# Second attention of a two-layer kernel: rotary rows of the next group exchanged and turned in two halves, at lower steps of the group

## The reference, cut to what matters

```python
q = rmsnorm(hidden_states @ wq_a.T, q_a_ln_w) @ wq_b.T       # 192 per head: 128 nope + 64 rotary
q_nope, q_pe = (q[..., :NOPE], q[..., NOPE:])
q_pe = apply_rope(q_pe, cos, sin)                            # x * cos + rot(x) * sin
q_abs = jnp.einsum('bhsd,hdc->bhsc', q_nope, q_absorb)       # 64 latent rows per head
scores = (jnp.einsum('bhsc,btc->bhst', q_abs, kv) + jnp.einsum('bhsd,bxtd->bhst', q_pe, k_pe)) * SCALE
attn = jax.nn.softmax(jnp.where(causal, scores, finfo.min), axis=-1)
x = jnp.einsum('bhst,btc->bhsc', attn, kv)                   # then the output projection
```

## Time and profile before

| what | us |
|---|---|
| median of 3 runs (1600.1 to 1606.49) | 1603.35 |
| the profiled execution | 1605.04 |
| its span in the profile | 1603.5 |

### The profile page before, as it was taken

One profiled execution on the slowest core, in us unless ns is written; L12 is line 12 of the kernel. 1 busy time (PEld: TensorE's weight loads), 2 busy tenths in 40 slices (PEclk: granted clock), 3 DMA queues, 4 the chain that ended last, 5 costly groups with the idle time before them and its releaser, 6 DMA issues. The chain is left out here.

```text
span 1603.5 us, 22609 instructions
## 1 busy us (share of the span) xinstructions
PE 1262.6 (79%) x7428; PEld 893.8 (56%) x7428; DVE 895.1 (56%) x2331; ACT 734.5 (46%) x1668; POOL 520.2 (32%) x556
## 2 busy tenths in 40 slices
PE   2675729888888838677699999997575999999977
PEld 1564714433333317466576666765564677777656
DVE  6656538766666533343666666661243666666640
ACT  1544403555454620452566666650153666666640
POOL 0221233333233110040355555530050555555520
PEclk8797955888777968788899999998797999999998
DMA  2213187554453049301111111005102111111005
GB/s 78 109 60 123 56 99 64 55 59 58 51 59 37 22 153 269 112 2 63 47 37 37 37 37 37 27 14 158 49 1 85 25 39 38 39 39 39 18 28 157
DMA packets 133157, 101.02 MB, mean 63 GB/s; under 512 B 48240, under 2 KB 120368, under 8 KB 132784
## 3 DMA queue, kind: packets, MB, share of 16 engines
q1 hardware_dynamic: 132000, 98.53, 27.4%
q10 hardware_dynamic: 1040, 1.05, 0.2%
HBM read 56.30 MB, written 34.87 MB: 57 GB/s over the span
## 5 line engine op out<-in xcount | busy, mean ns | idle before, releaser
L748 POOL TENSOR_SCALAR a_p<-a_p,a_rl 128x128 f32<-128x128 f32 (+7 forms) x256 | 215.6, 842 | 400.1 <-DVE a_rl L690 400.1
L731 ACT ACTIVATE a_p<-psum,a_nm 128x128 f32<-128x128 f32 (+7 forms) x256 | 189.5, 740 | 107.5 <-DVE a_nm L684 106.9
L1225 ACT ACTIVATE a_pt<-psum 128x512 f32<-128x512 f32 (+3 forms) x384 | 166.9, 492 | 154.3 <-PE psum L1098 152.8
L1088 PE MATMUL psum<-a_op_k,a_op_q 64*128 64x512 f32 (+3 forms) x384 | 162.6, 510 | 52.9 <-POOL a_op_k L1023 32.1
L781 PE MATMUL psum<-ident,a_p 128*128 128x128 f32 x1152 | 170.1, 275 | 31.8 <-DVE a_pt L717 31.8
L803 PE MATMUL psum<-a_pt,v 128*64 128x256 f32 (+1 forms) x1280 | 158.9, 370 | 1.1 <-ACT a_ot L817 1.1
L781 PEld LDWEIGHTS psum<-ident,a_p 128*128 128x128 f32 x1152 | 129.6, 140 | 53.5 <-issue 48.3
L684 DVE CUSTOM_DVE_ANT_0 psum<-psum,mask_a 128x128 f32<-128x128 f32 (+3 forms) x128 | 63.8, 499 | 149.4 <-PE psum L766 149.3
L1098 PE MATMUL psum<-a_op_q,a_op_k 64*128 64x512 f32 (+3 forms) x384 | 134.7, 455 | 0.0
L715 ACT ACTIVATE a_pt<-psum 128x256 f32<-128x256 f32 (+2 forms) x192 | 87.4, 455 | 94.8 <-PE psum L781 93.8
L1088 PEld LDWEIGHTS psum<-a_op_k,a_op_q 64*128 64x128 f32 x384 | 79.6, 235 | 90.3 <-issue 32.3
(11 more groups left out here) (257 smaller groups left out, 2810.7 us busy)
## 6 DMA issues: line engine op xcount, KB each, us to landing
a_swap<-a_raw SPq DMA_DIRECT2D x64, 128.0 KB, 2.3
ot_d<-a_ot SPq DMA_DIRECT2D x16, 512.0 KB, 2.6
o_ot<-ot_d SPq DMA_DIRECT2D x16, 512.0 KB, 6.2
a_raw_q<-qk_d SPq DMA_DIRECT2D x48, 128.0 KB, 5.1
a_raw_k<-qk_d SPq DMA_DIRECT2D x48, 128.0 KB, 9.5
a_wf<-wf_d SPq DMA_DIRECT2D x16, 384.0 KB, 3.2
qk_d<-p_stage_h SPq DMA_DIRECT2D x8, 512.0 KB, 2.7
qk_d<-p_stage_l SPq DMA_DIRECT2D x8, 512.0 KB, 3.4
```

The costliest lines, as they stand in the source:

```text
L731: e.activation(s.p[:, t % NPB, 0:(i + 1) * P], C.score[t % 2][:, 0:(i + 1) * P], ACT.Exp, scale=-1.0, bias=s.nm[:, k:k + 1], accum_out=s.l ...
L748: e.tensor_scalar(s.p[:, t % NPB, 0:(i + 1) * P], s.p[:, t % NPB, 0:(i + 1) * P], s.rl[:, k:k + 1], 1.0, ALU.mult, ALU.mult).then_inc(s.no ...
L1088: e.matmul(bank_a("score", g, k)[:, 0:k1 - k0], q[rows(hd), hd % 2, i * P:(i + 1) * P], kk[rows(hd), hd % 2, k0:k1], start=True, stop=True ...
L1225: e.activation(pt[:, k // G0 % NPT, hd, off:HALF], bank_b("score", g, k)[:, off:HALF], ACT.Exp, scale=-1.0).then_inc(exped, 1)
```

## The change

The rotary rows are handled in two halves of 512 tokens from the exchange on: SP issues eight DMAs of half the size instead of four, the first four as soon as the first half of `raw` is there. POOL's six operations go half by half (`swap` times sine, `raw` times cosine, sum; then the same for the second half). ACT's high part and DVE's rest of the rotary rows are each cut in two halves: four instructions of 64x512 instead of two of 64x1024. The group has 8 increments of `qhi` and `qlo` instead of 6. The tables put PE's pieces at steps 0, 1, 3, 5 (from 0, 2, 4, 6), ACT's at 0, 1, 3, 5, 6, 9 (from 0, 2, 4, 6, 12, 13), DVE's at 4, 6, 7, 10 (from 5, 7, 13, 14) and POOL's at 2 to 7 (from 4 to 9).

```diff
-        swapped = ph.sem("swapped")
+        swapped = [ph.sem("swapped0"), ph.sem("swapped1")]
...
             else:
-                hd = k - 4
-                r = PE_ROWS[hd]
-                e.wait_ge(roped, g * 6 + 6)
-                e.activation(q[u][hd][0][r, :], raw[r, :], ACT.Copy).then_inc(qhi, 1)
+                half = k - 4
+                t = slice(half * HALF, (half + 1) * HALF)
+                e.wait_ge(roped, g * 6 + 3 * half + 3)
+                for hd in range(2):
+                    r = PE_ROWS[hd]
+                    e.activation(q[u][hd][0][r, t], raw[r, t], ACT.Copy).then_inc(qhi, 1)
...
         def prep_dve(e, g, u, k):
...
+            e.wait_ge(qhi, g * 8 + 2 * (k - 1))
+            half = k % 2
+            t = slice(half * HALF, (half + 1) * HALF)
+            for hd in range(2):
+                if k < 4:
                     r = LAT_ROWS[hd]
-                    e.tensor_tensor(q[u][hd][1][r, t], place(g, k)[r, :], q[u][hd][0][r, t].bitcast(F32),
-                                    ALU.subtract).then_inc(qlo, 1)
-            else:
-                hd = k - 4
-                r = PE_ROWS[hd]
-                e.wait_ge(qhi, g * 6 + 5 + hd)
-                e.tensor_tensor(q[u][hd][1][r, :], raw[r, :], q[u][hd][0][r, :].bitcast(F32),
-                                ALU.subtract).then_inc(qlo, 1)
+                    whole = place(g, k)[r, :]
+                else:
+                    r = PE_ROWS[hd]
+                    whole = raw[r, t]
+                e.tensor_tensor(q[u][hd][1][r, t], whole, q[u][hd][0][r, t].bitcast(F32), ALU.subtract).then_inc(qlo, 1)
 
         def rotate(e, g, k):
 
-            t = slice((k % 2) * HALF, (k % 2 + 1) * HALF)
-            if k < 2:
-                e.wait_ge(swapped, (g + 1) * 64)
+            half, part = k // 3, k % 3
+            t = slice(half * HALF, (half + 1) * HALF)
+            if part == 0:
+                e.wait_ge(swapped[half], (g + 1) * 64)
                 e.tensor_tensor(swap[:, t], swap[:, t], st[:, t], ALU.mult).then_inc(roped, 1)
-            elif k < 4:
-                e.wait_ge(raw_out, g * 2 + 2)
+            elif part == 1:
+                e.wait_ge(raw_out, g * 2 + half + 1)
...
-        AT_PE = {0: 0, 2: 1, 4: 2, 6: 3}
-        AT_ACT = {0: 0, 2: 1, 4: 2, 6: 3, 12: 4, 13: 5}
-        AT_DVE = {5: 2, 7: 3, 13: 4, 14: 5}
-        AT_POOL = {4: 0, 5: 1, 6: 2, 7: 3, 8: 4, 9: 5}
+        AT_PE = {0: 0, 1: 1, 3: 2, 5: 3}
+        AT_ACT = {0: 0, 1: 1, 3: 2, 5: 3, 6: 4, 9: 5}
+        AT_DVE = {4: 2, 6: 3, 7: 4, 10: 5}
+        AT_POOL = {2: 0, 3: 1, 4: 2, 5: 3, 6: 4, 7: 5}
...
                 def exchange(g):
 
-                    e.wait_ge(raw_out, (g + 1) * 2)
-                    for r in range(0, P, 64):
-                        e.dma_start(swap[r:r + 32, :], raw[r + 32:r + 64, :]).then_inc(swapped, 16)
-                        e.dma_start(swap[r + 32:r + 64, :], raw[r:r + 32, :]).then_inc(swapped, 16)
+                    for half in range(2):
+                        t = slice(half * HALF, (half + 1) * HALF)
+                        e.wait_ge(raw_out, 2 * g + half + 1)
+                        for r in range(0, P, 64):
+                            e.dma_start(swap[r:r + 32, t], raw[r + 32:r + 64, t]).then_inc(swapped[half], 16)
+                            e.dma_start(swap[r + 32:r + 64, t], raw[r:r + 32, t]).then_inc(swapped[half], 16)
```

More of the change, by code:

```diff
@@ L1744, in prep_pe @@
                 if later:
-                    e.wait_ge(qlo, g * 6)
+                    e.wait_ge(qlo, g * 8)
             elif not later:
@@ L1750, in prep_pe @@
             else:
-                e.wait_ge(qhi, g * 6 + 2)
-                e.wait_ge(qlo, g * 6 + 2)
+                e.wait_ge(qhi, g * 8 + 2)
+                e.wait_ge(qlo, g * 8 + 2)
             c = k % 2
@@ L1767, in prep_act @@
                 if later and k == 0:
-                    e.wait_ge(qhi, g * 6)
-                    e.wait_ge(qlo, g * 6)
+                    e.wait_ge(qhi, g * 8)
+                    e.wait_ge(qlo, g * 8)
                 t = slice(k * HALF, (k + 1) * HALF)
@@ L1778, in prep_act @@
             else:
-                hd = k - 4
-                r = PE_ROWS[hd]
-                e.wait_ge(roped, g * 6 + 6)
-                e.activation(q[u][hd][0][r, :], raw[r, :], ACT.Copy).then_inc(qhi, 1)
-        def prep_dve(e, g, u, k):
[L1786 to L1789, removed]
-                    r = LAT_ROWS[hd]
-                    e.tensor_tensor(q[u][hd][1][r, t], place(g, k)[r, :], q[u][hd][0][r, t].bitcast(F32),
-                                    ALU.subtract).then_inc(qlo, 1)
-            else:
-                hd = k - 4
-                r = PE_ROWS[hd]
-                e.wait_ge(qhi, g * 6 + 5 + hd)
-                e.tensor_tensor(q[u][hd][1][r, :], raw[r, :], q[u][hd][0][r, :].bitcast(F32),
-                                ALU.subtract).then_inc(qlo, 1)
+                half = k - 4
@@ L1877, in slot @@
                         g = t // PREP
-                        e.wait_ge(qhi, (n * 2 + g + 1) * 6)
-                        e.wait_ge(qlo, (n * 2 + g + 1) * 6)
+                        e.wait_ge(qhi, (n * 2 + g + 1) * 8)
+                        e.wait_ge(qlo, (n * 2 + g + 1) * 8)
                     softmax_pe(e, C, s, n, t, later, score, value, KL)
```

## The result

| | median us (lowest to highest, runs) |
|---|---|
| before | 1604.92 (1600.10 to 1609.41, 4) |
| after | 1632.95 (1627.90 to 1634.14, 4) |

The ratio is 1.0169 [1.0131, 1.0207]: slower, by 28.0 us of the two medians; whether it is more or less than 2% is left open by the interval. The profiled execution took 1627.9 us with a span of 1626.3, which is 22.8 more than before.

The account below looks back on a forecast made before the run. PE was taken as the bound, idle 2.10 us a group. Per group -0.64 + 0.2 + 1.4 + 0.4 = +1.36, over 14 groups +19.0, less 1.6 at batch starts, gave 1621 us; range 1600 to 1634.

Parts of the forecast that it names:

- Step 14's wait goes: PE's wait in step 14 for DVE's copy, late behind step 13's long subtraction, disappears: -0.64 us per group.
- Output copy: PE's value product of step 5 waits for ACT's output copy, queued behind two latent copies: +0.2 us per group.
- Step 13's scores: DVE's rotary subtractions at step 10 delay step 11's minimum, so step 13's scores wait: +1.4 us per group.
- the port at step 10: DVE's subtraction and POOL's multiplication exclude each other at step 10: up to 0.8 us, within a +0.4 term.
- Two of the signs: Step 13's scores wait 1.5 us or more; DVE is never idle between the minima of steps 10 and 11.
- The port at step 7: DVE's second subtraction at step 7 can meet POOL's multiplication of step 6: up to 0.4 us, within +0.4.
- The group: A group takes about 41.2 us instead of 39.80, +1.36, with PE still busy 37.7.
- The start of each batch: PE's wait ahead of each batch falls from 10.70 to 9.9 us: gain 0.8 per batch, 1.6 in all.
- The first group: Each batch's first group has other early steps but runs as the others from step 8: counted at +1.36 us.
- faster: Rival, chance 0.14: extra work fits at step 11's minimum, old waits go and no new one comes: 1590 us.
- Worse: Rival, chance 0.17: POOL's last rotation is late, ACT waits 0.6 us, with the full port term: 1640 us.
- No change: Rival, chance 0.22: the new wait at step 13 about equals the old one at step 14: about 1602 us.

Follow-up runs that it names:

- e4: Kernel before with only the early projection steps of PE, ACT and DVE, rotary rows whole at their old steps: 1610.36 us, ratio 1.004.
- e6: Kernel before with two added 64x512 DVE subtractions from PSUM into a spare buffer at step 10: 1617.05 us, ratio 1.007.
- e5: Kernel after with the second rotary half's two subtractions at step 10 reading their first operand from PSUM instead of SBUF: 1636.71 us, one run.
- e1: Kernel after with the second rotary half moved back to ACT step 12 and DVE step 13: 1618.95 us, ratio 1.009.
- e3: Kernel after with all four step tables put back to those of the kernel before, leaving the cut in halves: 1627.79 us, ratio 1.0145.
- e7: Kernel after with the second rotary half moved to ACT step 13 and DVE step 14: 1625.86 us, ratio 1.015.
- e8: Kernel after with PE's pieces at old steps, first rotary half at ACT 5 and DVE 6, second at 13 and 14: 1629.70 us, ratio 1.0157.
- e12: e8 with DVE's subtractions placed ahead of the reciprocal in each step: 1624.36 us, ratio 1.0152.
- e10: e3 with DVE's subtractions placed ahead of the reciprocal in each step: 1604.00 us, ratio 1.0022.
- e2: Kernel after with only DVE's second rotary half moved back from step 10 to step 13: 1620.45 us, one run.
- e9: Kernel after with DVE's subtractions placed ahead of the reciprocal in each step: 1632.21 us, one run.

## Why the prediction came out as it did

The direction and the mechanism of the group were right. The range of 1600 to 1634 holds the measured 1632.95 by only 1 us, and the forecast's own narrower range, 1612 to 1632, doesn't hold it; that the wider one does is luck in part, since two costs below stood in no term. (By its own terms that range's upper end should read 1635: 14 x (-0.64 + 0.2 + 1.6 + 1.2) - 1.6 is +31.4.) The change was forecast at +17.4 us and came out at +28.0 between the medians, so the sum was short by 11; the median of before itself stands 1.6 us higher with the fourth run. Step by step:

- **Step 14's wait goes (-0.64).** Right: it is gone, and the wait at the group's start stayed (1.39 where 1.3 was foretold), since it hangs on the minimum of step 15.
- **Output copy (+0.2).** Right: 0.25 in the kernel after, 0.24 in e4 alone.
- **Step 13's scores (+1.4), and the port at step 10 (part of +0.4).** Together the wait grew from 0.17 to 1.38, +1.21, where both terms would give up to 1.8. The cause is right: e6 makes a wait of 1.13 in the kernel before with DVE work alone, and e5 takes only the port away and loses 0.36 of the group. A part of what I put on step 13 had been paid before: the scores of step 12 now wait 0.18 for the exponential of step 10. The new waits for exponentials are +1.39 together, where the two terms gave 1.8. Two of the signs failed in size: the wait was to be 1.5 us or more, and DVE was to be never idle between the minima of steps 10 and 11, but it stood 0.60 us waiting for ACT, where the sum itself had 0.39.
- **The port at step 7.** The second subtraction took 0.96 instead of 0.69, and no wait of PE in a middle group follows from it. In the first group it does (below).
- **The group.** 41.16 was forecast, 41.20 came, partly because two errors cancel. PE's idle time rose from 2.10 to 3.30 us, +1.20 where +1.36 was forecast (the waits named above, 0.10 more at the group's start and 0.11 before the transposes of step 12), and PE's busy time rose from 37.70 to 37.90, where I had left it as it was.
- **The start of each batch (-0.8).** Right: the wait ahead of the first score is 9.97, against 10.70 and 9.9 foretold; the whole start got 0.7 shorter.
- **The first group (the step that failed).** I wrote that it "has other early steps, but from step 8 on it runs as the others", and gave it +1.36. The two took +3.9 and +3.8, so 5 of the 11 us are here. Of these, +2.9 stood by the exponential of step 8 already. e4 shows that the early steps of the pieces alone make +1.0 to there and some +2.0 over the group; e1, which has the early steps and the first rotary half at step 7 but nothing at step 10, takes 3.5 more than before. So step 10, which I did count, is the smallest part. The waits are for exponentials, such as this one:

```profile
789.30 0.50 PE L766 MATMUL psum<-k0h,a_q00h 128*128 128x512 f32 x1 [0.99 <-ACT a_p L731]
```

  Between +1.0 and +2.9 lies the first rotary half at step 7. In the kernel after, the minimum of step 8 follows its two subtractions without a gap; in e4, which has none there, it follows the reciprocal of step 7 without a gap:

```profile
788.50 0.69 DVE L1798 TENSOR_TENSOR a_q10l<-a_raw,a_q10h 64x512 fp32r<-64x512 f32 x1
...
789.22 0.96 DVE L1798 TENSOR_TENSOR a_q11l<-a_raw,a_q11h 64x512 fp32r<-64x512 f32 x1
...
790.10 0.67 DVE L681 TENSOR_REDUCE a_part<-psum 128x1 f32<-128x512 f32 x1
```

  So in the first group DVE has no room at step 7 either. The middle of the group was the only one that I read; the first group has no scores of an earlier group to work off, and the pieces and the rotation come into it while the softmax is still filling. About 0.4 us of its +3.9 is the clock (my estimate): the granted clock rose to the 2.4 GHz level 4.69 us after the group's first scores, where it was 3.85 before, and until then it is at half of that. Which piece makes each of the other waits stays open.
- **Clock falls (in no case of mine).** 3.2 us in this execution; the next section has them. The other 0.5 of the three long groups is the port at step 10, as shown above.
- The rest of the distance, to the medians, is what lies between executions: the terms above give 27.1, and the medians differ by 28.0.

Of the rivals, "faster" was to be decided at the minimum of step 11, and e6 shows that there is no room there. "Worse" rested on a late rotation: it ended 0.52 us before ACT took up its result (917.01 and 917.53), and the forecast had put that slack at 0.5. "No change" needed a step-13 wait of some 0.8 (0.17 + 0.64), and it is 1.38.

## What the hardware showed beyond what I expected

**Who gets the port between two instructions.** One long subtraction of 64x1024 beside a waiting POOL multiplication took 1.22 us, undisturbed, and POOL 1.94. The same data in two of 64x512 took 0.69 + 1.39 (e1, e3), 0.69 + 1.50 (e3, step 14), and POOL 1.41. So a POOL multiplication that waits gets the port when DVE's instruction ends, though DVE's next one is due 0.03 us later. The other way round is in the kernel after at step 7, between two instructions of POOL:

```profile
912.26 0.97 POOL L748 TENSOR_SCALAR a_p<-a_p,a_rl 128x384 f32<-128x384 f32 x1 [0.65 <-DVE a_rl L690]
...
912.81 0.96 DVE L1798 TENSOR_TENSOR a_q01l<-a_raw,a_q01h 64x512 fp32r<-64x512 f32 x1
...
913.21 1.72 POOL L1809 TENSOR_TENSOR a_raw<-a_raw,a_ct 128x512 f32<-128x512 f32 x1
```

DVE's second subtraction, which waits since 912.81, ends at 913.77, and POOL's rotation behind the multiplication takes 1.72 us where it takes 1.27 undisturbed. In both cases the engine that waits gets the port at the end of the other's instruction, although the other's next one follows without a gap.

**The clock.** The granted clock fell from the 2.4 GHz level to the 1.2 GHz level for some 3 us inside the attention, twice in the kernel after. One fall came right after the wait at step 13's scores:

```profile
964.84 0.80 PE L766 MATMUL psum<-k0h,a_q00h 128*128 128x512 f32 x1 [1.38 <-ACT a_p L731]
965.43 0.63 PE L766 MATMUL psum<-k0h,a_q00l 128*128 128x512 f32 x1
965.86 0.63 PE L766 MATMUL psum<-k0l,a_q00h 128*128 128x512 f32 x1
```

The second and third start 0.43 us apart, where the same ones are 0.22 or 0.23 apart elsewhere. In the 5.4 us up to 965.40 PE had been busy for 3.46. The other groups of this kernel have the same wait at the same place and no fall there; the second fall, at 1060.4, stands near the start of the last group of batch 0, behind that group's wait of 1.39. Each fall made its group 1.3 to 1.7 us longer. The four kernels with four or five falls are those in which PE waits in step 15 (1.06, 1.51, 1.52 and 0.75 us in e3, e7, e8 and e12); e10, with 0.30 there, has none. The kernel after has two falls and no such wait, and e1, e2, e6 and e9, with waits of 1.0 to 1.4 us in steps 13 or 14, have none, nor has e5. So the place of the wait may matter more than its length, but what decides isn't settled by these profiles, one of each kernel. What they do show is the price: e7 and e8 have shorter middle groups than e1, and still their two attentions take 629.6 and 634.7 us together, against 628.4.

## What to carry to other kernels

Before moving work to an idle engine's "free" place, look at the loop of the step where it lands. If the engine that bounds already waits, however shortly, for the chain that passes there, each us put into it is a us lost, less what the engine still idles just there, whatever the engine's busy share: DVE was busy for two thirds of the group, and 1.37 us of work in e6 cost 0.92. A DVE operation on two SBUF operands beside POOL shouldn't be cut in two, unless what releases POOL comes behind both parts; and that order has to be looked at in every step, for in e9 it moved a subtraction into another POOL instruction and cost more than it saved. And read the first and the last turn of a loop apart from the middle: here the first held 5 of the 11 us that the forecast lacked.
